# Output products of two head groups in one bank: five blocks of a sample made into two

## The reference

```python
attn = jnp.einsum('bqd,bkd->bqk', q * scale, k)
rel_h = jnp.einsum('bhwc,hkc->bhwk', qr, Rh)
rel_w = jnp.einsum('bhwc,wkc->bhwk', qr, Rw)
attn = attn.reshape(B * nh, H, W, H, W) + rel_h[:, :, :, :, None] + rel_w[:, :, :, None, :]
attn = jax.nn.softmax(attn.reshape(B * nh, HW, HW).astype(jnp.float32), axis=-1)
out = jnp.einsum('bqk,bkd->bqd', attn, v)
out = out @ proj_w.T + proj_b
```

## Time and profile before

| | |
|---|---|
| median of three runs | 1974.27 us |
| profiled execution: time | 1973.15 us |
| profiled execution: span from first to last instruction | 1971.3 us |
| PE matmul busy | 1904.9 us (97%), 34944 instructions |
| PE weight load busy | 1558.5 us (79%) |
| DVE busy | 1436.1 us (73%) |
| ACT busy | 1364.7 us (69%) |
| POOL busy | 713.3 us (36%) |
| granted PE clock | 0.996 of full speed |
| the chain of work that ended last | PE 93%, issue 3%, DVE 2% |
| output products L543 | 6144 instructions, 388.7 us busy |
| DMA | 197.86 MB, mean 100 GB/s |

### The profile page before, as it was taken

How to read it: one execution, slowest core, us unless ns; L and a number is a source line. 1 busy time by engine, 2 the same in 40 slices (tenths; PEclk the granted TensorE clock), 3 DMA queues, 4 the chain that set the end, 5 groups by cost and what they waited for, 6 DMA issues and landing times.

```text
span 1971.3 us, 85928 instructions
## 1 busy us (share of the span) xinstructions
PE 1904.9 (97%) x34944; PEld 1558.5 (79%) x34944; DVE 1436.1 (73%) x3566; ACT 1364.7 (69%) x3201; POOL 713.3 (36%) x1796
## 2 busy tenths in 40 slices
PE   0799999999999999999999999999999999999998
PEld 0688888888888888888888888888888888888885
DVE  6477777777777777777777777777777777777774
ACT  0277777777777777777777777777777777777775
POOL 0333433334334334334334333343343343343331
PEclk9999999999999999999999999999999999999999
DMA  1434444444444444444344344444444444444430
GB/s 38 101 93 110 103 100 110 103 102 108 104 100 109 103 102 107 102 107 105 100 110 104 99 110 106 100 104 108 100 107 104 101 108 102 107 104 100 112 97 23
DMA packets 142177, 197.86 MB, mean 100 GB/s; under 512 B 26455, under 2 KB 109656, under 8 KB 141786
## 3 DMA queue, kind: packets, MB, share of 16 engines
q1 hardware_dynamic: 141786, 192.36, 39.3%
HBM read 97.74 MB, written 57.80 MB: 79 GB/s over the span
## 4 chain that ended last, share of the span: by engine, by line
PE 93%; issue 3%; DVE 2%; POOL 1%; ACT 0%; DMA 0%; POOLq 0%; SPq 0%; DVEq 0%; ACTq 0%
PE ps_m L402 24%; PE ps_max L511 17%; PE ps_o L543 17%; PE ps_sc L524 13%; PE ps_m L463 10%; PE ps_m L477 6%; PE ps_m L419 2%; PE ps_m L487 2%; PE ps_m L468 1%; PE ps_m L425 1%; DVE k_st L658 0%; POOL yo L837 0%; DVE v_st L651 0%; POOL xn L814 0%; POOL xn_lo L827 0%
## 5 line engine op out<-in xcount | busy, mean ns | idle before, releaser
L701 DVE TENSOR_REDUCE mx<-ps_max 98x2 f32<-98x392 f32 x1536 | 834.9, 558 | 237.3 <-PE ps_max L511 223.4
L574 ACT ACTIVATE probs<-ps_sc 98x392 f32<-98x392 f32 x1536 | 735.4, 496 | 216.8 <-PE ps_sc L524 171.8
L511 PE MATMUL ps_max<-k_st,q_st 124*98 124x196 f16 x3072 | 538.1, 257 | 0.6 <-DVE mx L701 0.3
L524 PE MATMUL ps_sc<-q_st,k_st 125*98 125x196 f16 x3072 | 511.7, 247 | 0.6 <-ACT probs L574 0.5
L511 PEld LDWEIGHTS ps_max<-k_st,q_st 124*98 124x98 f16 x3072 | 293.8, 125 | 200.1 <-issue 157.6
L543 PE MATMUL ps_o<-probs,v_st 98*32 98x196 f32 x6144 | 388.7, 340 | 2.0 <-issue 1.2
L524 PEld LDWEIGHTS ps_sc<-q_st,k_st 125*98 125x98 f16 x3072 | 320.9, 124 | 3.4 <-ACT probs L574 1.8
L752 DVE TENSOR_TENSOR rel_hl<-ps_m,rel_hi 128x504 f16<-128x504 f32 (+1 forms) x384 | 216.2, 563 | 85.5 <-ACT rel_hi L619 85.5
L785 POOL TENSOR_TENSOR msq<-mv 96x2 f32<-96x2 f32 x128 | 24.6, 192 | 630.5 <-DVE mv L727 630.5
L619 ACT ACTIVATE rel_hi<-ps_m,is_lo 128x504 f16<-128x504 f32 (+1 forms) x384 | 225.7, 588 | 31.6 <-PE ps_m L463 31.3
L463 PE MATMUL ps_m<-q_st,rel_st 64*32 64x36 f16 (+1 forms) x14336 | 238.0, 208 | 0.2 <-DVE gsm L767 0.2
(11 more groups left out here) (72 smaller groups left out, 3051.3 us busy)
## 6 DMA issues: line engine op xcount, KB each, us to landing
q_st<-q_dram SPq DMA_DIRECT2D x128, 294.0 KB, 3.9
k_st<-k_dram SPq DMA_DIRECT2D x256, 147.0 KB, 3.9
q_dram<-qk_hl SPq DMA_DIRECT2D x128, 147.0 KB, 2.6
k_dram<-qk_hl SPq DMA_DIRECT2D x128, 147.0 KB, 2.8
q_st<-rel_hl SPq DMA_DIRECT2D x256, 73.5 KB
q_st<-rel_hl SPq DMA_DIRECT2D x256, 64.3 KB
xa<-in_x SPq DMA_DIRECT2D x64, 147.0 KB
x<-yo SPq DMA_DIRECT2D x64, 147.0 KB
```

The lines of the kernel that those rows point to most:

```text
L511: last = nc.tensor.matmul(ps_max[head % 2][0:HT, h * TOK:h * TOK + TOK], q_st[u.n % QB][0:R_MAX, head, h, :], k_st[u.n % QB][0:R_MAX, head ...
L524: last = nc.tensor.matmul(ps_sc[head % 2][0:HT, kt * TOK:kt * TOK + TOK], k_st[u.n % QB][0:STACK, head, kt * HT:kt * HT + HT], q_st[u.n % ...
L574: nc.scalar.activation(probs[head][:, :, :], ps_sc[head % 2][0:HT, 0:2 * TOK].rearrange("p (k t) -> p k t", k=2), ACT.Exp, scale=1.0 / (QS ...
L701: nc.vector.reduce_max(mx[u.r % 2][:, head, :], ps_max[head % 2][0:HT, 0:2 * TOK].rearrange("p (q k) -> p q k", q=2), axis=AX.X).then_inc( ...
```

## The change

The bank `ps_o` takes two groups side by side: 196 columns for the first, 196 for the second. The eight heads of groups 0 and 1 are computed in one block at place 56 (slot 8, 32 instructions), the four heads of group 2 in another at 60 (slot 0, 16 instructions). Slots 4, 7, 11 and 1 have no output products any more. ACT makes two copies a unit, one of 392 columns for both groups in slot 9 and one of 196 columns in slot 1. `s_o` counts two per unit; `s_o_ps` still counts three, one per group.

```diff
--- before.py
+++ after.py
@@ -247,7 +247,8 @@
         LEAD, TAIL = 2, 6
         MAX_AT, EXP_AT = 30, 47
 
-        PV_AT = {(0, 0): 52, (0, 1): 52, (1, 0): 55, (1, 1): 56, (2, 0): 59, (2, 1): 61}
+        PV = ((0, 1), (2,))
+        PV_AT = (56, 60)
         O_LATER = 1
 
         JOBS = [(-10, "xT", 1, (s_xT, 1, 1)),
@@ -469,7 +470,7 @@
                                         ident[0:HT, 0:HT]).then_inc(s_mT_ps, 1)
                 elif name == "ot":
 
-                    pe.wait_ge(s_o, u.n * GROUPS + GROUPS)
+                    pe.wait_ge(s_o, u.n * len(PV) + len(PV))
                     bank_free(pe, unit, name)
                     for h in range(2):
                         for g in range(GROUPS):
@@ -529,21 +530,20 @@
                     for name in ORDER:
                         job(name, unit, s, layer)
 
-                    for (g, kt), at in PV_AT.items():
-                        u = due(unit, s, at)
+                    for i, groups in enumerate(PV):
+                        u = due(unit, s, PV_AT[i])
                         if u:
-                            n = u.n * GROUPS + g
-                            if kt == 0:
+                            if i == 0:
                                 wait(pe, s_v, u.n + 1)
-                                wait(pe, s_p, u.n * HEADS + HG * g + HG)
-                                wait(pe, s_o, n)
-                            for j in range(HG):
-                                head = HG * g + j
-                                p = probs[head]
-                                last = nc.tensor.matmul(ps_o[32 * j:32 * j + 32, 0:TOK],
-                                                        v_st[u.n % VB][:, kt, head_of(head), :], p[:, kt, :],
-                                                        start=kt == 0, stop=kt == 1)
-                            if kt == 1:
+                            wait(pe, s_p, u.n * HEADS + HG * groups[-1] + HG)
+                            wait(pe, s_o, u.n * len(PV) + i)
+                            for n, g in enumerate(groups):
+                                for kt in range(2):
+                                    for j in range(HG):
+                                        head = HG * g + j
+                                        last = nc.tensor.matmul(ps_o[32 * j:32 * j + 32, n * TOK:n * TOK + TOK],
+                                                                v_st[u.n % VB][:, kt, head_of(head), :],
+                                                                probs[head][:, kt, :], start=kt == 0, stop=kt == 1)
                                 last.then_inc(s_o_ps, 1)
 
             run(pe, iteration)
@@ -556,13 +556,14 @@
             def iteration(unit, layer):
                 for s in range(HEADS):
 
-                    for g in range(GROUPS):
-                        u = due(unit, s, PV_AT[g, 1] + O_LATER)
+                    for i, groups in enumerate(PV):
+                        u = due(unit, s, PV_AT[i] + O_LATER)
                         if u:
-                            act.wait_ge(s_o_ps, u.n * GROUPS + g + 1)
+                            act.wait_ge(s_o_ps, u.n * GROUPS + groups[-1] + 1)
                             wait(act, s_ot_ps, u.n - 1)
-                            nc.scalar.copy(o_sb[u.r % 2][:, g, :].rearrange("p (k r b) -> p k r b", r=2, b=SIDE),
-                                           ps_o[:, 0:TOK].rearrange("p (k b r) -> p k r b", r=2, b=SIDE))\
+                            nc.scalar.copy(o_sb[u.r % 2][:, groups[0]:groups[-1] + 1, :]
+                                           .rearrange("p g (k r b) -> p (g k) r b", r=2, b=SIDE),
+                                           ps_o[:, 0:len(groups) * TOK].rearrange("p (k b r) -> p k r b", r=2, b=SIDE))\
                               .then_inc(s_o, 1)
                     head = head_at(EXP_AT, s)
                     u = due(unit, s, EXP_AT + head)
```

## The result

The changed kernel takes 2040.14 us (median of 4 runs, 2039.53 to 2040.35) against 1974.03 for the kernel before (a median of 4 as well): ratio 1.0335, 95% interval 1.0323 to 1.0348. It is 3.4% slower; 2.6% (2025 us) was forecast, within a range of 1990 to 2042.

The account below looks back on a forecast made before the run. PE was taken as the bound, DVE and ACT just behind; per period +0.73 us in stretch B less 0.30 in stretch A gives +0.43, times 124 = +53, less 2 in the last iterations: 2025 us, range 1990 to 2042.

Parts of the forecast that it names:

- PE's price of a block: PE time of output products: 0.33 us of streaming per 8 instructions, plus 0.26 for entering and leaving their arrangement.
- Stretch A: PE from the last qk0 product (slot 4) to g (slot 8): 6.20 us shrinks to 5.90, giving 0.30.
- the g wait: PE held before g (slot 8) until DVE's second rel cut frees bank 2: about 0.37 us a period.
- the mT wait: PE held before mT until DVE's second q/k cut frees bank 1: 0.17 us a period.
- Rival 1, PE alone,: Waits at mT and g don't bind, each sample gives 0.67 us: faster, time 1889; chance 10%.
- The price of 0.26 us for going in and out of a block: On PE, a block after an ordinary matmul pays 0.26 us for entering and leaving the four-column arrangement, beside streaming.
- Stretch B: PE from g (slot 8) to the next last qk0 product: grows by 0.73 us, with nothing found to hide it.
- The ends: Outside the 124 full iterations: the last few, without qk0, gain 3 x 0.67, so -2 us.
- Costed at nothing: Side effects given no cost: ACT's two-group copy (0.49 us), later DVE slots, xn_lo and rel-row DMAs.

Follow-up runs that it names:

- the kernel before with both edits: The kernel before the change, with oT and rel1 in bank 0, rel0 in bank 2, and slot 4's statistics done in slot 3: 1968.77 us, ratio 0.9976.

## Why the prediction was right

- **PE's price of a block** held. The block of 32 takes 1007.45 - 1005.98 = 1.47 us (1.46 forecast), so passing to the next group's columns costs nothing; the block of 16 takes 0.81 (0.80). Late proof: where no wait is left, the variants come to 14.20, 14.07 and 13.94 us (14.17, 14.03 and 13.95 worked out).
- **Stretch A gives 0.30** held to the hundredth. The 5.90 us that the first iteration with output products showed is the length in the changed kernel. Four edits show the order: the g wait taken away alone, oT and g together, the mT wait alone, and all three (oT alone was not run). oT and mT hang on the same DVE work, g on the chain from mT over rel1, ACT and DVE. The forecast called DVE's work without a pause the reason that A can't shrink further. That is so only with the releases as they stand: with g in bank 0 the same DVE work lets A shrink to 1003.59 - 998.05 = 5.54 us.
- **Rival 1, PE alone,** fell here, and comes true as soon as the releases are out of the way. The price of 0.26 us for going in and out of a block is borne out by the variants without steady waits, and what fewer blocks save comes only where PE is the bound. The Trainium skill (TensorEngine Tiling (Array Packing), Key Properties) says that a change of the tiling mode drains TensorE; the periods agree with a price for each change, but no run shows that it is a drain.
- **The size** was 15 us short. Two terms were mis-sized. Stretch B grew by 0.78 instead of 0.73: after a wait, g takes 1005.98 - 1005.75 = 0.23 us to the next work instead of 0.19, and the last 0.01 is the long block. A period grew by 0.48 instead of 0.43, which makes 6 us. The ends were wrong in sign: -2 us forecast, +7 measured, of which 4.6 in the iteration of the fill, nearly all of it at half clock behind the two waits, and 2.8 in the last iterations, where I gave the blocks of slot 4 no cover to lose, though oT waits for DVE's division there. The sum was made for the steady stretch and its result carried to the ends without reading them.
- **Costed at nothing:** the copy of 392 columns takes 0.48 us (0.49 forecast), and nobody waits for it; DVE in slots 11 to 3 holds nobody up; xn_lo and the rel rows come in time.

## What to carry to other kernels

In a software pipeline whose bound engine shows no waits, ask of each piece of its work what other engines finish meanwhile: a stretch in which it waits for releases from a second engine can't be shortened below the chain of these releases, and work moved out of it is paid twice, as waits there and as length elsewhere. An iteration of the fill, in which the bound engine lacks part of its work, can show that chain's length directly (here 5.90 us, the same to the hundredth in the changed kernel). When grouping saves switches, put the groups where the waits would be, or first move the release (a bank, an earlier statistic), and remove all links of a chain of waits before judging one.

## What the runs showed that I had not expected

- Two edits that bring 58 and 20 us singly bring 145 together, and 4.5 without the change.
- Two idle gaps of 1.0 and 1.2 us within 5 us of PE's filling iteration were followed by 10 us at half clock (granted 0.52 and 0.50). That the gaps brought the fall is argued from their order, not shown: the variant with g in bank 0 was idle for 1.0 of the 5 us before as well and kept the full clock, the one with only the earlier statistics had a gap of 1.2 us at g (102.90) and lost it (granted 0.54 from 105 to 110). In the kernel before with both edits these 10 us had no idle time at all:

```profile
105.00:115.00 10.00, 10.00 (x192) 8.23 (x189) 7.92 (x21) 7.48 (x18) 2.23 (x6) 1.00 0.31 74
```
